# Queries scaled on GpSimd before their transposes, row maximum subtracted inside the score banks, one exponential instruction per chunk, and a new order of the work on five engines

## The reference

```python
qkv = x @ Wqkv                       # 128 -> 3 x (16 heads x 64)
q = l2norm(q) * qs ; k = l2norm(k) * ksc
q = q * cos * scale + rotate_half(q) * sin * scale
k = k * cos * inv   + rotate_half(k) * sin * inv
sim  = einsum('bhwie,bhwje->bhwij', bq, bk2) * QK_SCALE    # windows of 32 queries, 64 keys
sim  = where(mask, -finfo.max, sim)
attn = softmax(sim, -1)
out  = einsum('bhwij,bhwje->bhwie', attn, bv2)
x = out @ Wo + x
a, gate = split(layernorm(x) @ W1 + b1) ; x = (a * gelu(gate)) @ W2 + b2 + x
```

## Time and profile before

| what | value |
|---|---|
| median of 3 timed runs | 3912.69 us (3912.33 to 3920.5) |
| profiled execution | 3949.71 us, its span 3947.9 us |
| instructions in the span | 154738 |
| busy share of PE, PEld, DVE, ACT, POOL | 85%, 66%, 68%, 81%, 60% |
| granted TensorE clock, mean over the span | 0.962 |
| DMA moved | 272.84 MB, mean 69 GB/s |
| chain that ended last | PE 62%, ACT 20%, issue 13%, DVE 2% |

### The profile page before, as it was taken

How to read it: one execution, slowest core, us unless ns; L and a number is a source line. 1 busy time by engine, 2 the same in 40 slices (tenths; PEclk the granted TensorE clock), 3 DMA queues, 4 the chain that set the end, 5 groups by cost and what they waited for, 6 DMA issues and landing times.

```text
span 3947.9 us, 154738 instructions
## 1 busy us (share of the span) xinstructions
PE 3373.5 (85%) x64080; PEld 2589.6 (66%) x64080; DVE 2676.7 (68%) x5196; ACT 3201.0 (81%) x5968; POOL 2370.0 (60%) x1960
## 2 busy tenths in 40 slices
PE   6888888888888888887677888889888888888886
PEld 4666766766676667665335667667666667667664
DVE  4776777776666776765446666777766767777675
ACT  5898888888888888886227888888888888898883
POOL 5676666666666666663006666666666666666661
PEclk8999999999999999999778999999999999999998
DMA  2232232232232232232002322332232232232221
GB/s 82 75 83 69 74 81 72 75 78 72 71 83 68 70 86 64 76 80 58 6 0 61 80 69 70 77 79 70 75 80 71 74 77 75 75 77 69 69 64 34
DMA packets 207434, 272.84 MB, mean 69 GB/s; under 512 B 55700, under 2 KB 101648, under 8 KB 206736
## 3 DMA queue, kind: packets, MB, share of 16 engines
q1 hardware_dynamic: 206736, 262.94, 26.3%
HBM read 60.35 MB, written 1.05 MB: 16 GB/s over the span
## 4 chain that ended last, share of the span: by engine, by line
PE 62%; ACT 20%; issue 13%; DVE 2%; SPq 1%; POOL 1%; DMA 0%; DVEq 0%; ACTq 0%; POOLq 0%
PE PS L329 16%; ACT PR L728 9%; PE PS L377 6%; PE PS L439 5%; PE PS L486 5%; PE PS L378 5%; PE PS L379 5%; PE PS L495 5%; PE PS L463 5%; PE PS L521 3%; PE PS L431 2%; ACT PT L737 1%; ACT OT L756 1%; ACT L728 1%; ACT VS L749 1%
## 5 line engine op out<-in xcount | busy, mean ns | idle before, releaser
L1176 POOL TENSOR_TENSOR V<-RAWQK,TAB 128x512 f32<-128x512 f32 x768 | 971.3, 1287 | 936.1 <-PE PS L329 660.2
L728 ACT ACTIVATE PR<-PS,NB,RN 128x64 f32<-128x64 f32 x3072 | 930.6, 449 | 3.4 <-DVE NB L959 2.8
L377 PE MATMUL PS<-WH,XH 128*128 128x512 f32 x1152 | 519.3, 451 | 36.0 <-POOL XL L1158 24.1
L463 PE MATMUL PS<-V,PT 64*32 64x64 f32 x24576 | 344.9, 226 | 224.3 <-issue 223.8
L329 PE MATMUL PS<-EYE,V 128*128 128x128 f32 x3072 | 413.9, 279 | 92.3 <-ACT PR L728 91.5
L378 PE MATMUL PS<-WH,XL 128*128 128x512 f32 x1152 | 472.8, 410 | 2.5 <-issue 2.5
L379 PE MATMUL PS<-WL,XH 128*128 128x512 f32 x1152 | 472.4, 410 | 1.7 <-issue 1.7
L463 PEld LDWEIGHTS PS<-V,PT 64*32 64x32 f32 x24576 | 281.5, 106 | 286.9 <-issue 282.7
L1209 POOL TENSOR_TENSOR V<-V,U 128x1024 f32<-128x1024 f32 x192 | 453.6, 2362 | 14.9
L1202 POOL TENSOR_TENSOR V<-V,U 128x1024 f32<-128x1024 f32 x192 | 454.8, 2369 | 0.0
L329 PEld LDWEIGHTS PS<-EYE,V 128*128 128x128 f32 x3072 | 359.4, 143 | 136.0 <-issue 107.7
(11 more groups left out here) (150 smaller groups left out, 6913.6 us busy)
## 6 DMA issues: line engine op xcount, KB each, us to landing
V<-VS SPq DMA_DIRECT2D x3072, 64.0 KB
ROTB<-c_rot SPq DMA_DIRECT2D x192, 128.0 KB, 2.4
WSTAGE<-wqkv SPq DMA_DIRECT2D x33, 512.0 KB, 3.8
WO<-wo SPq DMA_DIRECT2D x12, 512.0 KB, 3.8
W<-w SPq DMA_DIRECT2D x12, 341.0 KB, 3.1
QKS<-qks SPq DMA_DIRECT2D x12, 128.0 KB, 3.7
W<-w SPq DMA_DIRECT2D x12, 114.0 KB
VS<-wqkv SPq DMA_DIRECT2D x2, 512.0 KB, 4.2
```

The costliest lines, as they stand in the source:

```text
L377: pe.matmul(o, XH[:, p, :], WH[:, w, cols], start=True, stop=False)
L463: mm = pe.matmul(PS[WIN * w:WIN * (w + 1), B_O + r, j * DH:(j + 1) * DH], PT[DH * r:DH * (r + 1), j, WIN * w:WIN * (w + 1)], V2[DH * r:DH ...
L728: ins = act.activation(PR[:, 2 * j + r, :], PS[:, B_S + r, j * 2 * WIN:(j + 1) * 2 * WIN], ACT.Exp, bias=NB[:, c % 2, h:h + 1], scale=RN[: ...
L1176: ins = pool.tensor_tensor(paired(V[:, k])[:, :, :, h * half:(h + 1) * half], split(RAWQK[:, k])[:, :, :, (1 - h) * half:(2 - h) * half], ...
```

## The change

Three computations change and the order of all pieces with them.

- `scale_queries` on GpSimd multiplies the rotated queries in V by their norms, before TensorE transposes them (it now waits for `q_scaled`).
- `row_max` on VectorE takes the maxima into SBUF (MX) and then subtracts them from the scores in their banks; the product NB is gone.
- `exponentials` on ScalarE is one instruction over 128x1024 instead of 16 over 128x64.
- The bank map is new: queries, transposed queries and scores now share banks 5 and 6; keys are in 3 and 4; values, weighed outputs and the output projection begin at bank 0. The `after(...)` waits follow it.
- The lists of pieces per step are new on TensorE, ScalarE, VectorE and GpSimd. Scores and weights come one step earlier relative to the projections.

The diff, cut to its core:

```diff
-B_Q = 3
-B_K = 5
-B_V = 1
+B_Q = 5
+B_K = 3
+B_V = 0
 B_TQ = 5
-B_TK = 3
+B_TK = 1
 B_S = 5
-B_P = 2
+B_P = 1
 B_O = 0
-B_TO = 2
-B_WO = 2
-B_F1 = 0
-B_F2 = 1
-B_F3 = 4
+B_TO = 0
+B_WO = 0
+B_F1 = 4
+B_F2 = 3
+B_F3 = 2
...
 def turn_queries(c):
-                    pe.wait_ge(q_turned, count(inv, c))
-                    after(use(exp_done, c - 1), use(uk_done, c), use(q_kept, c - 1))
+                    pe.wait_ge(q_scaled, count(inv, c))
+                    after(use(uq_done, c + 1), use(exp_done, c - 1), use(q_kept, c - 1))
...
-                for t in range(108):
-                    turn_weights(t - 3)
-                    ffn_third(t - 2)
-                    scores(t - 2)
-                    turn_outputs(t - 4)
-                    weigh(t - 3)
+                for t in range(107):
+                    keys(t)
+                    values(t - 1)
                     queries(t)
+                    turn_weights(t - 2)
                     project_out(t - 4)
+                    ffn_second(t - 1)
+                    turn_keys(t - 1)
                     turn_queries(t - 1)
-                    values(t - 1)
-                    keys(t)
-                    turn_keys(t - 1)
                     ffn_first(t - 1)
-                    ffn_second(t - 1)
+                    turn_outputs(t - 3)
+                    ffn_third(t - 1)
+                    scores(t - 1)
+                    weigh(t - 2)
...
 def exponentials(c):
-                    act.wait_ge(bias_done, count(inv, c))
+                    act.wait_ge(shifted, count(inv, c))
...
-                    for r in range(2):
-                        for j in range(NP_):
-                            h = r * NP_ + j
-                            ins = act.activation(PR[:, 2 * j + r, :], PS[:, B_S + r, j * 2 * WIN:(j + 1) * 2 * WIN], ACT.Exp,
-                                                 bias=NB[:, c % 2, h:h + 1], scale=RN[:, c % 2, h:h + 1])
-                    ins.then_inc(exp_done, 1)
+                    act.activation(PR[:, :, :].rearrange("p (j r) k -> p r j k", r=2),
+                                   rows(B_S).rearrange("p r (j k) -> p r j k", k=2 * WIN), ACT.Exp).then_inc(exp_done, 1)
...
 def row_max(c):
-                    dve.tensor_reduce(MX[:, :], rows(B_S).rearrange("p b (j k) -> p (b j) k", k=2 * WIN),
-                                      AX.X, ALU.max)
+                    s = rows(B_S).rearrange("p b (j k) -> p b j k", k=2 * WIN)
+                    dve.tensor_reduce(MX[:, :, :], s, AX.X, ALU.max)
                     dve.drain()
-                    held(exp_done, count(inv, c - 2))
-                    dve.scalar_tensor_tensor(NB[:, c % 2, :], MX[:, :], -1.0, RN[:, c % 2, 0:HEADS],
-                                             ALU.mult, ALU.mult).then_inc(bias_done, 1)
+                    dve.tensor_tensor(s, s, rep(MX[:, :, :], [P, 2, NP_, 2 * WIN], 3), ALU.subtract).then_inc(shifted, 1)
...
+                def scale_queries(c):
+                    if not live(c):
+                        return
+                    pool.wait_ge(norms, chain_count(inv, c))
+                    pool.wait_ge(q_turned, count(inv, c))
+                    rn = RN[:, c % 2, 0:HEADS].rearrange("p (r j) -> p j r", r=2).unsqueeze(3).broadcast_to([P, NP_, 2, DH])
+                    v = V[:, 0].rearrange("p (j r) d -> p j r d", r=2)
+                    pool.tensor_tensor(v, v, rn, ALU.mult).then_inc(q_scaled, 1)
...
                 for t in range(108):
+                    sin_keys(t - 2)
                     sin_queries(t - 2)
-                    sin_keys(t - 2)
+                    low_part(t - 1)
                     add_queries(t - 2)
-                    low_part(t - 1)
                     add_keys(t - 2)
+                    scale_queries(t - 2)
+                    ffn(t - 2)
                     table(t)
-                    ffn(t - 2)
```

More of the change, by code:

```diff
@@ L397, in keys @@
                     pe.wait_ge(xs_low, count(inv, c))
-                    after(use(q_kept, c - 1), use(exp_done, c - 2), use(uk_done, c - 1))
+                    after(second(c - 2), use(uk_done, c - 1), second(c - 3), second(c - 4))
+                    after(first(c - 2), use(uk_done, c - 1), first(c - 3), first(c - 4))
                     project(1, c, B_K).then_inc(k_raw, 1)
@@ L406, in values @@
                     pe.wait_ge(xs_low, count(inv, c))
-                    after(use(o_scaled, c - 2), second(c - 1), use(v_kept, c - 1), second(c - 2), second(c - 3))
-                    after(use(xb_done, c - 3), use(o_kept, c - 3), use(p_kept, c - 2), use(v_kept, c - 1))
+                    after(use(o_scaled, c - 2), use(o_kept, c - 3), use(xb_done, c - 4), use(v_kept, c - 1))
+                    after(use(o_scaled, c - 2), use(o_kept, c - 3), use(k_kept, c - 1), use(p_kept, c - 2), use(v_kept, c - 1))
                     project(2, c, B_V).then_inc(v_raw, 1)
@@ L428, in scores @@
                         return
-                    after(use(uk_done, c + 1), use(q_kept, c), use(exp_done, c - 1))
+                    after(use(q_kept, c), use(uq_done, c + 1), use(exp_done, c - 1))
                     for r in range(2):
@@ L457, in weigh @@
                     pe.wait_ge(v2_odd if c % 2 else v2_even, v2_count(inv, c))
-                    after(first(c + 1), use(o_scaled, c - 1), first(c + 0), first(c - 1))
-                    after(second(c + 1), use(v_kept, c + 1), use(o_scaled, c - 1), second(c + 0), second(c - 1))
+                    after(use(o_kept, c - 1), use(xb_done, c - 2), use(v_kept, c + 1), use(o_scaled, c - 1))
+                    after(use(o_kept, c - 1), use(k_kept, c + 1), use(p_kept, c), use(v_kept, c + 1), use(o_scaled, c - 1))
                     for j in range(NP_):
@@ L500, in ffn_first @@
                         return
-                    after(use(o_scaled, n - 2), first(n - 1), first(n - 2), first(n - 3))
+                    after(use(uk_done, n + 1), first(n - 1), first(n - 2), first(n - 3))
                     if q == 0:
@@ L515, in ffn_second @@
                     if q == 1 and 0 <= g - 1 < NGR:
-                        after(use(v_kept, n), use(o_scaled, n - 2), second(n - 1), second(n - 2), second(n - 3))
+                        after(use(uk_done, n + 1), second(n - 1), second(n - 2), second(n - 3))
                         if (g - 1) % NG == 0:
```

66 lines of the change are left out of this document (32 added, 34 removed).

## The result

The changed kernel takes 3979.38 us (median of 4 runs, 3957.07 to 3987.64), the kernel before 3916.6 on the same chip: a ratio of 1.0151, 95% interval 1.0108 to 1.0195. The change makes the kernel 1.5% slower; the forecast was 4% slower, 4075 us. The profiled execution took 3987.64 us with a span of 3985.9, which is 38 us more than the span before.

What follows compares the result with a forecast made beforehand. TensorE, waiting for its own code, was taken as the limit, with ScalarE close. Stall +192, clock +82, ScalarE waits -140 and new waits +30 gave +164 on 3949.7; less 37 for the median, 4075 us (range 3740 to 4210).

Steps and rivals of the forecast that it cites:

- the code stall: TensorE waiting for its next 256 instructions in scores and weighing, now adjacent: 1.0 us a chunk longer, +192 us.
- the two bare rows: Two trace samples of TensorE's stall with no output transposes covering the fetch: 2.44 and 2.01 us.
- The clock: TensorE at half clock behind long stalls, an event in half of the chunks at 1.6 us: +82 us net.
- ScalarE's waits: TensorE's waits for ScalarE, whose exponentials hold banks the query transposes want, would go: -140 us.
- new waits: Allowance for TensorE waiting on the new order's hand-overs through VectorE, GpSimd and ScalarE: +30 us (0 to 190).
- The passes: Predicted times: VectorE's subtraction 1.25 us, GpSimd's query scaling 2.37 to 2.6, ScalarE's single exponential about 1.03 to 1.1.
- What would show it: Profile signs: weighing idle 2.0 to 2.6 us, over 380 in sum; clock 0.93 to 0.97; period 19.4 to 19.8 us.
- rival 1: TensorE's code supply gets no worse and its waits for ScalarE go: -170 us, 3743 us, faster; chance 0.25.
- point of decision: Mean TensorE stall in the weighing under 1.9 us would decide for the faster outcome, 3743 us.
- Rival 2: TensorE's code stall grows but half-clock stretches do not: +46 us, 3960 us (3890 to 3990); chance 0.18.
- Rival 3: VectorE and GpSimd's hand-over chain after the weighing is late every chunk: 1 us a chunk more, 4265 us; chance 0.10.

Runs made afterwards that it cites:

- the spread order: Changed kernel reordered so output transposes and the second and third FFN steps stand between scores and weighing, other engines following: 4068.29 us, ratio 1.0371 to the kernel before.
- the FFN steps between: Changed kernel with first (three of four chunks) and last FFN step between scores and weighing, VectorE's row maximum ahead of its FFN piece: 3905.52 us, ratio 0.9972.
- the outputs inside: Changed kernel with the output transposes moved to the middle of the scores and the third FFN step between scores and weighing: 3977.08 us, ratio 1.0168.
- the weighing twice: Changed kernel with the 64 weighing matmuls issued twice into the same banks, the second set overwriting the first: 4931.04 us, one run.

## Why the prediction was right in its direction and wrong in its size

**The step that was mis-sized** is the code stall, "+1.0 us a chunk, +192 us". The mechanism is the one predicted: the transposes left the block in which they covered a fetch (2.47 us of work became 1.53), and the stall grew. But it grew by 0.66 us a block, and by 117 us over the span. I had taken 4.0 us for a block from two samples and held it fixed. The mean before was 3.77, and it fell to 3.49 after. Of the two bare rows, 2.44 us is in the top tenth of the idles before the weighing after, and 2.01 above their middle; their mean is 1.80. The trace shows where the fall sits. In the blocks that end in a stall (158 before, 180 after) the means are 3.90 us before, 1.26 until the transfer starts, 1.25 for the transfer and 1.39 from its end until TensorE goes on, and 3.55 after, 1.03, 1.15 and 1.36. Two thirds of the fall are the earlier start of the transfer; why it starts earlier stays open.

**The clock**, +82: measured +72, 100 half-clock stretches (forecast 96) at 1.8 us instead of 1.6. Today's loss was higher too, 108 instead of 72. The clock of the steady stretch, forecast 0.93 to 0.97, is 0.95.

**ScalarE's waits**, -140, **and new waits**, +30: the semaphore waits fell by 110, just their sum. That is luck between two terms: TensorE's waits for ScalarE fell by 113 over the span (136.9 to 23.9), all others rose by 3. Near zero they are as expected in the steady stretch.

**The passes:** the subtraction takes 1.23 us (forecast 1.25); GpSimd's query scaling 1.94, not 2.37 to 2.6; the exponential 1.03. ScalarE is at 67% of the steady stretch.

**What would show it:** the stall was to be 2.0 to 2.6 us in most chunks and above 380 us over the span; the idle before the weighing is 341 us over the span, 1.8 in the mean, and a third of the chunks have 2.0 to 2.6, so both signs failed. (From start to start it is 1.96; the 62 us in the scores were not part of the sign.) The period was to be 19.4 to 19.8; it is 19.0. With 117 for 192 the sum would have been +89 on the profiled execution, 4002 us after the same subtraction of 37; against 3979, 23 us remain. That this is so little is luck too: 10 are the clock's and 41 are those that the three columns have too much, but the profiled execution after lay 8 us above its median and not 37, which takes 29 back.

**The rivals:** rival 1, the supply gets no worse, is out: +117. Its point of decision, a mean stall in the weighing under 1.9 us, was met all the same, by the idle that the prediction's rows show (168.0 us in 94 places, 1.79), and the time still came out on the other side of before. The point lay too high: at 1.79 the stalls were 117 us longer and the clock was lower already. Rival 2, no more half clock, is out by its mechanism (61 to 100 stretches), though its 3960 lay nearer to the result than the forecast, and its range (3890 to 3990) holds it. Rival 3 is out for after: over the span its transposes of keys and queries wait 5.8 us for VectorE. Its chain shows in the spread order, at 0.4 us a chunk.

**What stays open:** in the spread order and with the FFN steps between, 131 and 64 us of the span are in none of the three columns. With the outputs inside it was the same, and the loads' wait for QT (218.5 against 67.2 us on PE) accounts for it. In the spread order the loads' wait for the scaled keys (73.8 against 29.1) accounts for some 40 of the 131; for the rest, and with the FFN steps between, no such row was found. The 41 us of after against before stay open, too. And no run has the new arithmetic in the old order, or the new order with the old arithmetic, so what each part of the change is worth alone is argued from the waits and not shown.

## What to carry to other kernels

Where TensorE runs many small matmuls in a row, count instructions, not time: look for idles "issue" at every 256th instruction, and place long instructions that must be done anyway between the dense bursts; the kernel with both FFN steps there has the lowest time of this case, if only by 0.3%. Before moving a piece, ask what it covers where it stands now (a fetch, a copy out of a bank, a wait for another engine), because an order that repairs one cover easily breaks the next. And price a relief by the engine's waits that it ends: 710 us less on ScalarE could be worth at most the 125 us (91.5 + 33.7 over the span) that TensorE had waited for it in the query and key transposes, and stalls and clock took 189 (117 + 72). Part of those waits came from banks shared with the exponentials, so the new bank map may have ended them as much as the faster ScalarE did.

## What the runs showed of the hardware

- Eight superfluous transposes a chunk, 192 us of work on TensorE, made a kernel 63 us faster.
- Code behaves as if one block ahead were all that is there: a burst of 256 short instructions (1.4 to 1.5 us of work) takes 3.5 to 3.9 us start to start (means of 3.49 from scores to weighing after, 3.88 wholly in the weighing with the weighing twice). In after that is about 1.0 us until the transfer of the next block starts, 1.14 for the transfer (the median in the stalls) and 1.37 until TensorE goes on. In the stalls of the spread order the transfer starts only 4.0 us behind the block's start.
- The granted clock falls to 0.50 behind such stalls in about half of the chunks (100 stretches after), and nearly in every one where two of them follow each other: 199 stretches for 192 chunks with the weighing twice.
- Sixteen exponentials of 128x64 with `scale` and `bias` read from tiles take 4.85 us a chunk, without them 1.97.
- A GpSimd multiplication of 128x1024 by an operand broadcast along 64 took 1939 ns, the addition of two full operands 2354 to 2378.
